# One block later for the next tokens' transposes, router product and low part in the experts' stage of a linear-attention block

## What is computed

```python
h = _layernorm(x, axis=-1) * (1 + cb) + sb
scores = jnp.maximum((h @ gate_W + gate_b) / TEMP, EPS)
p = jax.nn.softmax(scores, axis=-1)
_, topk_idx = jax.lax.top_k(p, 2)
...
comb = jnp.where(topk_mask, w, 0)          # w: clamped p over their sum
y = jnp.einsum('bsd,edf->bsef', h, expert_W) + expert_b
out = jnp.einsum('bsef,bse->bsf', y, comb) / 2
x = x + gb * out
```

## Time and profile before

| | |
|---|---|
| median of 3 runs | 3618.65 us (3607.57 to 3626.08) |
| profiled execution: time, span | 3621.35 us, 3619.6 us |
| PE busy over the span | 3264.2 us (90%) |
| DVE busy | 2613.1 us (72%) |
| ACT busy | 1754.8 us (48%) |
| POOL busy | 1226.6 us (34%) |
| mean granted TensorE clock | 0.983 |

### The profile page before, as it was taken

How to read it: one execution, slowest core, us unless ns; L and a number is a source line. 1 busy time by engine, 2 the same in 40 slices (tenths; PEclk the granted TensorE clock), 3 DMA queues, 4 the chain that set the end, 5 groups by cost and what they waited for, 6 DMA issues and landing times. The chain is left out here.

```text
span 3619.6 us, 129713 instructions
## 1 busy us (share of the span) xinstructions
PE 3264.2 (90%) x51114; PEld 2783.3 (77%) x51114; DVE 2613.1 (72%) x6866; ACT 1754.8 (48%) x4365; POOL 1226.6 (34%) x1057
## 2 busy tenths in 40 slices
PE   6898999999998998899999989989987999999998
PEld 5777777778787777777787777778775777777777
DVE  5676767666767767676666677767757888888887
ACT  4565656555665665555555666556542111111211
POOL 3333333343443333333333433333321222222222
PEclk9999999999999999999999999999998999999999
DMA  4222222222222222222222222222212111111110
GB/s 138 68 73 71 76 71 70 73 67 73 76 87 72 68 74 74 67 73 73 67 73 68 77 83 73 71 71 75 67 51 77 42 36 42 42 36 36 48 36 24
DMA packets 158631, 238.73 MB, mean 66 GB/s; under 512 B 30232, under 2 KB 82504, under 8 KB 157768
## 3 DMA queue, kind: packets, MB, share of 16 engines
q1 hardware_dynamic: 158024, 230.33, 19.8%
HBM read 194.58 MB, written 35.67 MB: 64 GB/s over the span
## 5 line engine op out<-in xcount | busy, mean ns | idle before, releaser
L442 POOL TENSOR_TENSOR oT_lo<-oT,oT_hi 128x512 fp32r<-128x512 f32 x256 | 332.0, 1297 | 1491.4 <-ACT oT_hi L526 1464.8
L543 ACT ACTIVATE kd_sb<-bank_scores,decay 128x64 f32<-128x64 f32 x2048 | 446.9, 329 | 655.0 <-PE bank_scores L741 652.6
L896 DVE SCALAR_TENSOR_TENSOR s_mid<-s_mid,lam_bc,bank_nums 128x65 f32<-128x65 f32 x1280 | 361.5, 282 | 46.9 <-DVE s_mid L896 1.4
L450 POOL TENSOR_TENSOR qs_sb<-lam_bc,qk_sb 128x512 f32<-128x512 f32 x256 | 333.9, 1304 | 157.1 <-PE bank_nums L725 119.5
L896 DVE SCALAR_TENSOR_TENSOR s_mid<-carry,lam_bc,bank_nums 128x65 f32<-128x65 f32 x256 | 72.3, 282 | 430.4 <-PE bank_dense L732 428.8
L741 PE MATMUL bank_scores<-qk_sb 64*64 64x128 f32 x8192 | 346.1, 274 | 29.5 <-issue 29.4
L508 ACT ACTIVATE qk_sb<-bank 128x512 f32<-128x512 f32 x512 | 318.0, 621 | 38.5 <-PE bank L582 21.3
L510 ACT ACTIVATE qk_sb<-qk_sb 128x512 f32<-128x512 f32 x512 | 324.2, 633 | 16.3
L915 DVE TENSOR_TENSOR_SCAN decay<-a_bc,eye 128x512 f32<-128x512 f32 x256 | 315.6, 1233 | 21.8 <-DMA a_bc<-rows_dram 21.8
L525 ACT ACTIVATE oT<-bank 128x512 f32<-128x512 f32 x256 | 153.1, 598 | 297.7 <-PE bank L707 297.1
L1247 DVE SCALAR_TENSOR_TENSOR acc<-bank_scores,comb,acc 128x256 f32<-128x256 f32 x512 | 230.7, 477 | 78.4 <-PE bank_scores L1161 77.5
(11 more groups left out here) (214 smaller groups left out, 9650.4 us busy)
## 6 DMA issues: line engine op xcount, KB each, us to landing
a_bc<-rows_dram SPq DMA_DIRECT2D x512, 128.0 KB, 2.9
lam_bc<-rows_dram SPq DMA_DIRECT2D x512, 128.0 KB, 2.9
x_in<-in_L_attn_x_dram SPq DMA_DIRECT2D x32, 512.0 KB, 6.3
x_res<-in_L_attn_x_dram SPq DMA_DIRECT2D x32, 512.0 KB, 3.9
x_dram<-x_res SPq DMA_DIRECT2D x32, 512.0 KB, 3.4
x<-x_dram SPq DMA_DIRECT2D x32, 512.0 KB, 3.3
out_dram<-x SPq DMA_DIRECT2D x32, 512.0 KB, 2.9
ew_raw<-in_L_ffn_expert_W_dram SPq DMA_DIRECT2D x8, 256.0 KB, 6.0
```

The source lines that it names most:

```text
L442: pool.tensor_tensor(oT_lo[:, u, :], oT32[:, :], oT_hi[:, u, :].bitcast(F32), ALU.subtract).then_inc(oT_lo_ready, 1)
L450: pool.tensor_tensor(qs_sb[:, na, :], lam_bc[na][:, :], q_sb, ALU.mult).then_inc(qs_ready, 1)
L543: ins = act.activation(kd_sb[:, t, hd * DH:(hd + 1) * DH], KTR[:, hd, t * CK:(t + 1) * CK], ACT.Copy, scale=decay[:, hd, t, CK - 1:CK])
L896: dve.scalar_tensor_tensor(dst, src, lam_bc[nb][:, (ch + 1) * CK - 1:(ch + 1) * CK], U[ch], ALU.mult, ALU.add).then_inc(state_step, 1)
```

## The change

PE's two transpose steps for the next group come behind blocks 1 and 2 instead of blocks 0 and 1, and the router's product behind block 3 instead of block 2. On DVE the low part comes behind the adds of block 2 instead of those of block 1. Nothing is added or taken away, and no other queue is written differently.

```diff
@@ PE, group
-                    if j < KT and exists(T + 1):
-                        transpose_h(T + 1, j)
-                    if j == KT and exists(T + 1):
+                    if 1 <= j <= KT and exists(T + 1):
+                        transpose_h(T + 1, j - 1)
+                    if j == KT + 1 and exists(T + 1):
                         gate(T + 1)
@@ DVE, group
-                adds(0, 2 * BLOCK_ADDS)
+                adds(0, ROUTE_BLOCK * BLOCK_ADDS)
                 if exists(T + 1):
                     h_low(T + 1, (s + 1) % 2)
-                adds(2 * BLOCK_ADDS, ROUTE_BLOCK * BLOCK_ADDS)
```

## The result

| | before | after |
|---|---|---|
| median of 9 runs | 3618.9 us | 3598.28 us (3589.84 to 3603.96) |
| profiled execution: span | 3619.6 us | 3602.2 us |
| mean granted TensorE clock | 0.983 | 0.986 |

The ratio is 0.9945, with a 95% interval of 0.9932 to 0.9959: the change makes the kernel faster by 20.6 us, 0.55%. Forecast were 3616.5 us and a range from 3601 to 3632. The direction of the sum (-2 us) was right, its size a tenth of what came; "faster by over 0.5%" had 6%.

What follows compares the result with a forecast made beforehand. Bound before was loop A with PE's 1.65 us wait for `xn`; after, loop B, also 26.95 us. Outside steady groups +5.7, clock falls -6.8, lost slack -1: -2 on 3618.65 gave 3616.5 us, range 3601 to 3632.

Steps and rivals of the forecast that it cites:

- loop A: The old bound: `xn`, transposes, blocks 1 and 2, product, block 3, DVE's `route` and adds back to `xn`; 26.95 us.
- loop B: Head of `route`, `comb_cols`, its transposes, block 0, biases, next transposes and blocks, product, next head; 26.95 us after the change.
- the new waits: PE was to wait 0.8 us before block 5 and about 0.7 before the transposes of `comb_cols`, each group.
- the falls of the clock: Four drops to 1.2 GHz behind the wait for `xn` were to go, 1.7 us each, -6.8 in all.
- R + 26.95: Sum from one head of `route`, at R, to the next in the changed kernel's steady groups: a 26.95 us period.
- The product to DVE, 0.21: Distance from the end of the router's product on PE to DVE's head of `route`, taken as 0.21 us.
- `route` without its waits, 12.74: DVE's time from head of `route` to `comb_cols`: 13.22 us less 0.48 of waiting for block 3.
- +2.1: First group: a further block in front of the product, less waits that go, was to add 2.1 us.
- +2.2: Seam between the loop's rounds: the added block, less 0.63 us by which `comb_cols` is taken up earlier, costs 2.2.
- The wait goes and nothing replaces it: Rival: PE runs without a gap, 25.15 us a group, -54 us, total 3565 us; 4%.
- POOL's hold falls elsewhere: Rival: `route`'s woven adds escape POOL's hold, 1.44 us less a group, total about 3575 us; 2%.
- The new waits bring the clock down: Rival: block 0 runs at 1.2 GHz behind the wait for `comb_cols`, 1.7 us a group, total 3668 us; 4%.

Runs made afterwards that it cites:

- e1: In the kernel before the change, only the router's product moved one block later, behind block 3; 3674.18 us, one run.
- e2: In the changed kernel, the low part put back between the adds of blocks 1 and 2 on DVE; 3603.62 us, one run.
- e4: In the changed kernel, the router's product put between the two halves of block 3; 3562.64 us, ratio to before 0.9845.
- e3: In the changed kernel, the router's product moved one block later still, behind block 4; 3724.06 us, one run.
- e5: In the changed kernel, both of POOL's results of a group start only when `xn` of the group after next is written; 3581.79 us, ratio 0.9886.
- e8: In the kernel before the change, only POOL's second result of a group moved behind the end of `xn`; 3561.25 us, ratio 0.983.
- e6: In the kernel before the change, both of POOL's results start only when `xn` is written; 3557.6 us, ratio 0.9827.

## Why the prediction was wrong

**Right:** what bounded before (loop A with the wait for `xn`); that the wait goes; that loop B takes over with the product at its head; where the new waits stand; that the low part ends before the product (1.16 us to spare); that the falls of the clock go. e1, e2 and e4 show the loop from three sides, e3 that each block in front of the product costs its full length.

**The step that failed** is the sum of loop B, "R + 26.95". Its terms against those of the group above:

| term | forecast | measured |
|---|---|---|
| `route` to `comb_cols` | 12.74 | 12.45 |
| to PE | 0.06 | 0.05 |
| transposes of it and block 0 | 3.24 | 3.28 |
| biases and block 1 | 3.36 | 3.28 |
| transposes, block 2, transposes, block 3 | 6.62 | 6.57 |
| product, and to DVE | 0.93 | 0.78 |
| period | 26.95 | 26.41 |

Two terms carry 0.44 us of the difference of 0.54.

*The product to DVE, 0.21.* It was taken from the first group, where the product took 1.04 us instead of 0.72, PE being at 1.2 GHz. After the change the same place still shows 0.21:

```profile
2734.13 1.04 PE L1179 MATMUL bank_dense<-gw,h 128*32 128x8 f32 x64 [0.87 <-ACT h L1125]
...
2735.38 0.18 DVE L1298 TENSOR_TENSOR sc<-bank_dense,gbias 128x32 f32<-128x32 f32 x1
```

but in the steady groups it is 0.06 (3130.62 to 3130.68), like `comb_cols` to PE. I had that value as an end of the range only. The difference of 0.15 us, 30 times, is 4.5 us.

*`route` without its waits, 12.74.* I had subtracted the 0.48 us that the timeline names. But DVE's instructions begin 0.08 us before the one in front ends by its record (in the changed kernel 3109.05 + 0.47 and 3109.44), so an instruction that need not wait starts 0.56 earlier, not 0.48. And there was a second wait, at the second half of block 6. The timeline of the loop's group does not mark it, since it is only 0.2 us there (the add starts 0.30 behind the instruction in front of it, 3119.11 and 3119.41, instead of 0.10); in the written-out groups it is 0.4. In the kernel before:

```profile
2794.25 0.39 PE L1161 MATMUL bank<-ew_hi,h_lo 128*128 128x512 f32 x1
```

```profile
2794.19 0.18 DVE L1319 TENSOR_TENSOR first<-first,second 128x32 f32<-128x32 f32 x1
2794.69 0.49 DVE L1247 SCALAR_TENSOR_TENSOR acc<-bank,comb,acc 128x256 f32<-128x256 f32 x1 [0.32 <-PE bank L1161]
```

and at the same place after, with the block long done:

```profile
2796.84 0.17 DVE L1319 TENSOR_TENSOR first<-first,second 128x32 f32<-128x32 f32 x1
2796.94 0.47 DVE L1247 SCALAR_TENSOR_TENSOR acc<-bank,comb,acc 128x256 f32<-128x256 f32 x1
```

The add comes 0.10 behind its forerunner's start instead of 0.50. So `route` had 0.77 us of waiting in the loop (13.22 to 12.45), not 0.48.

**The rest of the sum.** The 29 ordinary periods average (824.0 - 25.4 - 31.4) / 29 = 26.46 us instead of 26.95: -14.3 us. The prediction gave the written-out groups the loop's 26.95 as well; they run at 26.2 ((2839.4 - 2787.0) / 2), with 12.24 us from the head of `route` to `comb_cols` (2787.00 to 2799.24) instead of 12.45. The first period was 25.4 where +2.1 on 24.9 made 26.9. Here most of the 1.5 us is luck: PE starts this group at 1.2 GHz and was back at 2.4 GHz 19.5 us behind the first head before, and 16.4 us behind it after (the attention had come out 3.1 us longer), which is worth half of the 3.1 us. The period at the seam was 31.4 where +2.2 on 30.4 made 32.6: the two terms (0.44), PE's halt of 3.1 instead of 3.5 us, and some 0.45 that the forecast left out, since before the change DVE reached this head 0.66 us behind the product's end (3193.84 and 3194.50) and the new path meets it without that slack. Together the two are -2.8 us, and with the ordinary periods that is the 17 us between forecast and result within the phase. The four falls of the clock (-6.8) went as said.

**The range.** Its lower bound of the period, 26.80, replaced one of the two terms by its lower neighbour and left the other as exact. Both were readings of one row each, of the kind that errs to one side: a wait that is read too short and a distance that is read too long both made the new loop longer.

**The rivals.** "The wait goes and nothing replaces it" needed a `route` under 11 us and is out for the change, but e4 reaches PE's own pace by moving the product half a block. "POOL's hold falls elsewhere" was priced at -1.44 us a group; made true in e5 it gave 0.66, since the third loop takes over. "The new waits bring the clock down" did not happen with waits of 0.5 and 0.3 us; it took the 3.5 us of e3.

**POOL's hold.** The Trainium skill's rule (GPSIMD Engine Reference, Specifications) that GpSimd contends with VectorE's instructions with two SBUF inputs or in a two-port mode was only used for `route`. The wait that the change set out from is such a hold too, as e8 shows: `xn`'s instructions took 904 ns on the mean before and 407 in e8. They have one tensor input; whether they run in a two-port mode, and so fall under that rule, no run here shows. The low part has two inputs in SBUF and took 937 ns under POOL in e6 instead of 687, as the rule has it. POOL's second result does not start ahead of `ln_apply`, as the section on the kernel before says, but 0.27 us behind its first instruction (3123.93 and 3124.20 before; 3118.93 and 3119.20 after), and so it works beside the four of them. POOL in the group shown above (after):

```profile
3119.20 1.29 POOL L1092 TENSOR_TENSOR acc<-acc,gb 128x512 f32<-128x512 f32 x1 [0.76 <-DVE acc L1247]
3120.57 1.30 POOL L1094 TENSOR_TENSOR x<-x,acc 128x512 f32<-128x512 f32 x1
```

## What to carry to other kernels

A wait that is removed by moving work leaves the next loop through both engines to set the pace; add that loop up as well, and every loop that branches off it, before giving the wait's length as the gain. When taking a chain's length from a trace in which it waited, compare the start-to-start distances of its instructions with those of the same instructions where nothing is waited for, rather than subtract the idle times that are printed. And ask first why the awaited work is late: here a wait on POOL cost nothing and freed 60 to 66 us (e8 and e6, ratio 0.983 in both), three times what moving PE's work gave, and with it that move is a loss.

## Not expected of the hardware

- An instruction of DVE under POOL's work is held until POOL's instruction ends, rather than slowed. Four `xn` instructions took 3.42 us beside two POOL instructions of 1.3 us, and 1.38 without; two of the four take the usual 0.40 and two 1.4, and in the eleven groups before the change each of the 22 long ones ends 0.15 us behind a POOL instruction. The two of `route` end 0.05 behind one (after):

```profile
3108.85 1.29 POOL L1092 TENSOR_TENSOR acc<-acc,gb 128x512 f32<-128x512 f32 x1 [13.36 <-DVE acc L1247]
...
3109.44 0.74 DVE L1311 TENSOR_TENSOR first<-first,red 128x32 f32<-128x32 f32 x1
...
3110.22 1.28 POOL L1094 TENSOR_TENSOR x<-x,acc 128x512 f32<-128x512 f32 x1
...
3110.51 1.05 DVE L1313 SCALAR_TENSOR_TENSOR tmp<-first,prob 128x32 f32<-128x32 f32 x1
```

- The adds, which read one operand from PSUM, are not held: in e6 the 60 that lie wholly under a POOL instruction take 478 ns on the mean, the others 479.
- The wait that brings the clock down need not be long: some 1.7 us with transposes behind it did it in four groups before, and in about every second group of e1, 3.4 us in nearly every group of e3; waits of 0.5 and 0.2 us never did in the changed kernel's stage.
- The distance from PE's last matmul to DVE's first instruction is 0.06 us at 2.4 GHz, but 0.21 by the record where PE is at 1.2 GHz. Whether that is the true distance or how the matmul's end is modelled, no run here shows.
